# Attention with relative positions and a mixture of experts: the products ahead of the transposes in each TensorE step

## The reference, cut to what matters

```python
x = x + attn(layernorm(x))        # 8 batches, 512 tokens, width 128, 16 heads of 8
x = x + experts(layernorm(x))     # gated experts, 8 with the best 2 taken, and 2 shared

# attn
rel = tril(idx[:, None] - idx[None, :])
att = einsum('bhtd,bhsd->bhts', q, k) / sqrt(8) + einsum('bhtd,tsd->bhts', q, embk[rel])
att = softmax(where(causal, att, -inf))
y   = einsum('bhts,bhsd->bhtd', att, v) + einsum('bhts,tsd->bhtd', att, embv[rel])
return y @ w_proj
```

## Time and profile before

| what | value |
|---|---|
| median of 3 runs | 797.58 us (796.44 to 797.76) |
| profiled execution: its own time, span | 790.65 us, 788.9 us |
| TensorE busy | 705.4 us (89%) |
| VectorE busy | 588.3 us (75%) |
| ScalarE busy | 516.9 us (66%) |
| GpSimd busy | 255.8 us (32%) |
| mean granted TensorE clock | 0.97 |

### The profile page before, as it was taken

One profiled execution on the slowest core, in us unless ns is written; L12 is line 12 of the kernel. 1 busy time (PEld: TensorE's weight loads), 2 busy tenths in 40 slices (PEclk: granted clock), 3 DMA queues, 4 the chain that ended last, 5 costly groups with the idle time before them and its releaser, 6 DMA issues. The chain is left out here.

```text
span 788.9 us, 27137 instructions
## 1 busy us (share of the span) xinstructions
PE 705.4 (89%) x10368; PEld 511.1 (65%) x10368; DVE 588.3 (75%) x2036; ACT 516.9 (66%) x1032; POOL 255.8 (32%) x253
## 2 busy tenths in 40 slices
PE   3757779996989998988998988997999999999998
PEld 1545547775767677766777766775566666666665
DVE  6855667885878788888888878887367776776676
ACT  2576777885888777898887898877424434443331
POOL 9343355432545533445633535533000000000000
PEclk9897999998999999999999999999799999999999
DMA  9699999988688878778778678851000000000000
GB/s 305 230 277 287 329 271 291 299 268 253 220 250 264 292 229 249 239 217 268 232 230 253 211 239 252 260 160 47 2 22 27 27 1 27 28 15 0 14 15 14
DMA packets 116687, 140.32 MB, mean 178 GB/s; under 512 B 8848, under 2 KB 83088, under 8 KB 116368
## 3 DMA queue, kind: packets, MB, share of 16 engines
q1 hardware_dynamic: 116560, 138.59, 57.5%
HBM read 82.26 MB, written 56.30 MB: 176 GB/s over the span
## 5 line engine op out<-in xcount | busy, mean ns | idle before, releaser
L1041 DVE CUSTOM_DVE_ANT_0 ps<-ps,near 128x128 f32<-128x128 f32 (+3 forms) x512 | 244.8, 509 | 94.7 <-PE ps L812 63.1
L966 ACT ACTIVATE work<-ps,nmin 128x128 f32<-128x128 f32 (+3 forms) x512 | 249.8, 545 | 72.4 <-DVE nmin L1041 65.4
L824 PE MATMUL ps<-ident,work 128*128 128x128 f32 x1280 | 204.9, 280 | 13.9 <-issue 12.7
L824 PEld LDWEIGHTS ps<-ident,work 128*128 128x128 f32 x1280 | 159.0, 144 | 36.8 <-issue 18.9
L812 PE MATMUL ps<-kb,qb 128*128 128x128 bf16 (+3 forms) x512 | 131.5, 309 | 19.8 <-ACT work L966 15.9
L770 POOL TENSOR_SCALAR_AFFINE_SELECT work<-work 128x512 f32<-128x512 f32 x96 | 61.3, 638 | 242.2 <-ACT work L955 201.9
L1358 ACT ACTIVATE near<-ps 128x512 f32<-128x512 f32 x80 | 47.6, 595 | 136.6 <-PE ps L1323 136.5
L774 POOL TENSOR_TENSOR work<-work 128x512 f32<-128x512 f32 x96 | 124.3, 1295 | 8.0
L1026 DVE COPY work<-ps 128x512 f32<-128x512 f32 (+1 forms) x192 | 123.1, 641 | 1.0 <-PE ps L824 1.0
L1333 PEld LDWEIGHTS ps<-work,near 128*128 128x128 f32 x640 | 82.5, 191 | 34.3 <-issue 31.7
L841 PE MATMUL ps<-work,vb 128*9 128x128 f32 x2560 | 96.7, 279 | 0.8 <-ACT relS L944 0.8
(11 more groups left out here) (110 smaller groups left out, 629.6 us busy)
## 6 DMA issues: line engine op xcount, KB each, us to landing
near<-w_slots SPq DMA_DIRECT2D x96, 512.0 KB, 5.3
w_slots<-relS SPq DMA_DIRECT2D x128, 256.0 KB, 4.7
qk_rows<-work SPq DMA_DIRECT2D x36, 256.0 KB, 4.2
near<-w_slots SPq DMA_DIRECT2D x32, 256.0 KB, 4.6
w_slots<-near SPq DMA_DIRECT2D x8, 512.0 KB, 6.0
qk_rows<-y SPq DMA_DIRECT2D x9, 256.0 KB, 5.5
qb<-qk_rows SPq DMA_DIRECT2D x24, 96.0 KB
kb<-qk_rows SPq DMA_DIRECT2D x24, 96.0 KB
```

What stands on the lines that cost most here:

```text
L824: ins = nc.tensor.transpose(tp_ps[:, m % 2, n * P:(n + 1) * P], prob[:, m % PROBS, n * P:(n + 1) * P], ident[:, :])
L966: ins = nc.scalar.activation(prob[:, m % PROBS, h * wide:(h + 1) * wide], qk_ps[:, m % 3, h * wide:(h + 1) * wide], ACT.Exp, bias=nmin[:, ...
L1041: nc.vector.tensor_tensor_reduce(out=scores, in0=scores, in1=near[:, q % NEAR, a, 4 * P - wide:4 * P, r], scale=1.0, scalar=3e38, op0=ALU. ...
```

## The change

In each step of TensorE's program the loop over `OPS[m]` stands ahead of the transposes, no longer behind them. The scores of the next unit stay last. No other engine's program, no wait, no bank and no plan is touched.

```diff
                 for m in range(SLOTS):
+                    for kind, *what in OPS[m] if m else []:
+                        do[kind](*what)
                     if 0 <= m - 3 < NU:
                         tp(m - 3)
-                    for kind, *what in OPS[m] if m else []:
-                        do[kind](*what)
                     if m + 1 < NU:
                         qk(m + 1)
                     if m == NU + 2:
```

## The result

The changed kernel takes 823.24 us (median of 4 runs, 821.11 to 823.29) where the kernel before takes 797.53: a ratio of 1.032, 95% interval 1.030 to 1.034. Run again in a later batch, both unchanged, it was 824.86 against 797.81 us. The forecast was 820 us. Ratios leave out executions more than 1.5% above the fastest of their kernel, so in a widely scattered group they differ by some tenths of a per cent from the ratio of the medians.

What follows compares the result with a forecast made beforehand. TensorE was taken as the bound; waits at bank takes behind ScalarE (20 us) and VectorE (10 us), less 8 given back, net +22: 790.65 + 22 = 813 us profiled, 797.6 + 22 = 820 us median, range 801 to 834.

Steps and rivals of the forecast that it cites:

- The switch after the scores: TensorE, 172 steps whose narrow first operation now follows the scores: 0.1 us as after transposes, bounds 0 to -17 us, taken 0.
- From narrow to transposes: TensorE, transposes now right behind narrow products: priced as narrow products in front of scores, so no added cost.
- Takes behind ScalarE: 28 operations taking a bank ScalarE empties in the step before, behind its copy of late transposes: +20 us of TensorE waits.
- Takes behind VectorE: Operations taking a bank that VectorE's `normalise` reads behind `pT_copy` and `scores_min`: +10 us of waits.
- 8 us given back by `near`: VectorE's waits for `near` from memory shrink as transfers go on while TensorE waits: 8 us credited, at most 12.7.
- rival 2: 49 steps with a `rel` and no ScalarE copy: earlier `rel` shortens the way to `near`, -8 us, 790 us; chance 0.07.
- Steady steps 0: Row 2 steps with `av`: ScalarE's copy and `exp` released 0.9 us later, half a microsecond left, so 0.
- sign (e): Sign to look for in the profile after: row 2's steady stretch as long as before.
- rival 3: The 64 `av` steps in rows 2 and 3 each wait some 0.2 us for `exp`: +13, 833 us; chance 0.08.
- Rival 4: Waits in row 1 and the `rel` runs make TensorE's clock fall more: +6 to +10, 828 us; chance 0.10.
- Rival 1: Memory transfers, DMA 94% busy in row 1, swallow the waits: about 22 of 30 us go, 806 us; chance 0.13.
- rival 5: Whole kernel: the moves cancel and the change does nothing, 798 us; chance 0.06.

Runs made afterwards that it cites:

- Experiment 2: Changed kernel with ScalarE's copies of what the operations left put ahead of its copy of the transposes: 812.75 us, ratio 1.015 to the kernel before.
- experiment 7: Against the kernel before, only rel, yt, yb, pj ahead of the transposes, ScalarE's readers ahead of its transposes' copy: 801.34 against 800.95 us, ratio 1.002.

## Why the prediction was right, point by point

- *TensorE is the bound; an added wait is added to the end*: right. Waits of TensorE of 25 and 23 us in the two pairs came out as a longer loop, 33 and 28 us with its own work.
- *The switch after the scores costs what it costs after the transposes*: right, 0.1 us; the 17 us of the lower bound were not to be had. *From narrow to transposes as from narrow to scores*: wrong by 0.055 us, 183 times. It is the term that was mis-sized, 0 for an estimated 10 us. Both sides of a pair of neighbours had to be looked at; I bounded only one.
- *No transposes' wait is filled*: not shown by itself. They fell from 12.7 to 4.8 us, and by 11.5 in the repeated pair; that the takes in front absorb them fits, and no run separates it.
- *Takes behind ScalarE, +20 us*: measured after less before 9.6 (`yt` behind `rel`; 8 expected), 3.6 (`rel` behind `rel`; 5.9), 2.3 (`rv`; 2.7), 3.0 (`rel` behind `yb`; 3.5), in all 18.5. Experiment 2 shows the cause: with ScalarE's order turned, they go. Not foreseen: `av` behind a `rel` at 4.4 us more, most of it in one wait of 2.9, and `yb` for `rel_copy`, 1.5.
- *Takes behind VectorE, +10 us*: 10.3 us for L1059 and L1066 where there were 1.4, so +9. The wait at slot 139 is 0.33 where 0.5 was worked out. The parts are rougher than the sum: `yt` 1.3 (2 expected), `rel` behind `yt` in row 3 3.4 (4), in row 1 0.5 (1.8), `yb` 3.6 where it shared 2.2 with all the others.
- *8 us given back by `near`*: VectorE's wait fell by 7.9 and 8.5 us in the two pairs. That this is a gift of the longer steps, and not of `rel` coming earlier (rival 2), is argued from ScalarE's copy being later; experiment 7 comes nearest to a test: there `rel_copy` no longer stands behind the copy, as rival 2 asks, and no gain shows.
- *Steady steps 0*: not as long as before, so sign (e) failed. Between slots 264 and 288, where the kernel before has no wait, row 2 grew from 23.28 to 24.42 us, the same in both pairs (slots 176 to 200: 24.12 to 24.41 in the first pair, with a wait of 0.35 before, and 23.28 to 24.42 in the second). 13 switches are 0.7 of it; 0.33 is one wait of the scores for `exp`, the wait of rival 3, but once in 24 steps and not in each of the six with `av`. So rival 3 (+13) is out in size, not in kind. Rival 4, the clock: 0.98 in the loop in both. Out as well; the waits added did not make it fall. Rival 1 (806) gave back too much, rival 5 nothing.
- *The total*: 813 us for the profiled execution against 823.25, short by the 10 us of the switch. For the median 820 against 823.24 looks better than it is: the offset of 6.9 us from the profiled execution to the median did not carry over to the changed kernel, whose two numbers agree. That the forecast came within 3 us is luck in so far as this offset made up for most of the missing term; the net of the waits, 22 us forecast and 25 and 23 measured, is not.

## What to carry to other kernels

Where several engines walk the same list of steps in order, a block of work between two takes of a buffer is also the cover under which the reader empties it. Before moving it, list the uses whose buffer is read only one step earlier, follow the reader's own program order (here a copy of late transposes stood in front of the one that mattered), and price each as chain less cover; that list, not the count of moved steps, gave the loss. And price both sides of each new pair of neighbours on TensorE, not only the one that is moved in front.

## What the runs showed of the hardware

- fp32 transposes of 128 x 128 cost 0.055 us more per block right behind matmuls with 9 or 32 weight columns at column offsets, and not behind bf16 matmuls or other transposes (0.38 against 0.33 us for three, 0.49 against 0.44 for four). A bf16 score matmul in the same place is 0.01 us longer.
- Executions of the kernel before ranged from 785 to 803 us in 19 runs on one chip, the four of the first batch within 1.3 us. The quickest of the 19 had a mean granted clock of 0.975, the slowest 0.959. One profile is not the median: the trace that the sum was made against lay 7 us below it.
